# Weight roundings, low parts and loads in another order around the attention's first heads and two graph convolutions, and the second head's up-projection inside the first head

## The chip, the core and the metric

One NeuronCore of a Trainium2 chip runs the whole program. The time is the device time of one execution in microseconds (us), the median over several runs.

## The reference, cut to what matters

x is 256 nodes by 768 features in float32. Four stages follow one another, each `x = x + gnn(layernorm(x))`, `x = x + ffn(layernorm(x))`. Stages 0 and 1 hold a graph attention with 8 heads:

```python
h = (x @ W1).reshape(n, heads, C)            # up-projection, 768 -> 768 for each head
e = leaky_relu(a_s.h[src] + a_d.h[dst])      # edge scores
alpha = segment_softmax(e, dst)
out = segment_sum(h[src] * alpha, dst) + b1  # attention
h = elu(out)
out = gat(h, W2, heads=1)                    # down-projection over all 8 heads, one more attention
```

Stages 2 and 3 hold a graph convolution (`segment_sum((x @ W)[src] * norm, dst) + b`; in stage 3 behind a relational one over 34 edge types). The feed-forward parts of stages 2 and 3 begin with a router, `softmax(x @ router_w + b)`, beside their first weight matrix.

## The kernel before

**Products.** Every float32 product is made of three in a rounded format: hi x hi, lo x hi, hi x lo (`mm3`, L435). For each weight, ACT makes the rounded copy `w_hi` from the loaded `w_in` (`high`, L951), and DVE the low part `w_lo` = `w_in` - `w_hi` (`low`, L1278). PE waits for `w_low`. The same goes for activations: `xT_hi`/`xT_lo`, `h_hi`/`h_lo`, `hid_hi`/`hid_lo`, and the turned attention `aT_hi`/`aT_lo`.

**Weights.** A chunk is a 768 x 768 weight, in two parts of three row tiles. `w_in` holds one chunk: part p of load n is issued on SP (`load`, L301) when ACT and DVE have made `w_hi` and `w_lo` of part p of chunk n-1. `w_hi` and `w_lo` have two halves, which chunks take in turn (`half_of`).

**Attention.** In layer 0 an edge count runs first: a loop of 16 batches in which ACT and DVE build one-hot tiles (L1092, L1511) and PE multiplies them, with head 0's up-projection between. For each head (`gat` on every engine): up-projection into four PSUM banks (12 steps of six 384-column matmuls, tile m and row tile k), scores by four dot products on DVE (L1284), `spread` (PE, waits `scored`: puts the source scores in a row), masked maximum and exponentials on DVE and ACT, normalisation to `alpha`, `turn` (PE, L531, waits `normed`), `aT_hi` on ACT, `aT_lo` on DVE, attention (36 matmuls of 256 columns), ELU in three pieces (`kept`, `exponential`, `rounded` on ACT; `negative`, `unit`, `remainder` on DVE), down-projection (12 steps of 512 + 256 columns). In the loop of heads, PE's order is: up(h), down(h-1) steps 0 to 2, spread(h), down 3 to 8, turn(h), down 9 to 11, attention(h). Head 0 has no down-projection to put between, and fills with matmuls on a tile of zeros (`seed`): 25 between spread and turn, 5 behind the turn. The order on each engine is the order of the code.

**Edge table.** A table of 9.4 MB in DRAM collects edge counts for stage 3. One DMA on SP clears it (L316), and POOL then adds with indirect DMAs (L394), one batch of four a head. For each batch DVE marks first occurrences (`batch_firsts`, L1408, last of them `again`), and waits for POOL to have taken the batch before (`b_taken`, L383).

**Convolutions.** `gcn` (PE): sums over neighbours, then the product with W for tile 0 and tile 1 of the nodes, with the transpositions of tile 0's result (`turn_tile`, L474) before the last two steps of tile 1. On DVE `gcn_out` adds a tile to the stream x (L1702), takes statistics, scales it to `neg_b`; the next product (`gated` in stage 2, `nodes` in stage 3, each with router steps of 8 columns) needs its transposes. The router's weight `rw`, its bias and three to five rows, broadcast by DMAs on ACT's queue (L1177, L1244, L934), all count on one semaphore, for which the rounding of `rw` waits.

## Time and profile before

| | |
|---|---|
| median of 3 runs | 1367.29 us (1366.14 to 1368.6) |
| profiled execution | 1367.41 us, span 1365.6 us, mean granted TensorE clock 0.984 |
| PE busy | 1293.2 us, 95% |
| DVE busy | 995.1 us, 73% |
| ACT busy | 643.3 us, 47% |
| POOL busy | 213.7 us, 16% |
| largest stretch of PE in the chain | 527.50 us, the relation loop |

A page of the profile gives busy times and groups of instructions. Times in the timelines are us from the start of the span. L12 is line 12 of the kernel before. A bracket at the end of a row is the idle time of that engine before it, with what ended it. PE's rows overlap, since matmuls are pipelined.

### The profile page before, as it was taken

The page shows a single profiled execution, that of the slowest core. Times are in us where ns is not written, and L with a number is a line of the kernel's source. Part 1 is how long each engine was busy: PE and PEld are TensorE (multiplying, and loading weights), DVE is VectorE, ACT ScalarE, POOL GpSimd, SP SyncE. Part 2 cuts the span into 40 slices and gives each one's busy share as a digit, 9 for nine tenths or more (in the row PEclk, how much of TensorE's full clock was granted, in tenths as well). Part 3 has the DMA queues.
Part 4 walks back from the last instruction along what each step waited for, and adds up shares of the span by engine and source line. Part 5 has one row for each costly group of instructions (what it writes and reads, how often), then busy time and mean ns, then how long its engine had stood idle before and what let it go on. Part 6 is the DMA issues. An engine that isn't in the chain of part 4 may idle for free.

```text
span 1365.6 us, 21196 instructions
## 1 busy us (share of the span) xinstructions
PE 1293.2 (95%) x7823; PEld 1144.5 (84%) x7823; DVE 995.1 (73%) x1633; ACT 643.3 (47%) x832; POOL 213.7 (16%) x160
## 2 busy tenths in 40 slices
PE   6899999988899999988878999999999999999997
PEld 5699999965799999967667888898888988889886
DVE  6888888987688888975757755666556665566666
ACT  5666565554466555544334433433334333343342
POOL 0034433340034443440000000000000000000200
PEclk9999999998999999998989999999999999999999
DMA  9855665653355665644244554445544455443540
GB/s 303 262 185 169 192 212 174 197 130 120 104 197 169 177 209 191 185 107 132 79 138 162 201 184 154 154 163 192 183 154 154 164 190 183 154 154 139 199 114 32
DMA packets 103875, 227.33 MB, mean 166 GB/s; under 512 B 16710, under 2 KB 34950, under 8 KB 103840
## 3 DMA queue, kind: packets, MB, share of 16 engines
q1 hardware_dynamic: 72924, 192.43, 40.3%
q10 hardware_dynamic: 20980, 31.78, 8.6%
q0 software_dynamic: 9936, 2.66, 2.0%
q8 instruction: 21, 0.34, 0.1%
q14 instruction: 14, 0.11, 0.0%
HBM read 216.56 MB, written 10.29 MB: 166 GB/s over the span
## 4 chain that ended last, share of the span: by engine, by line
PE 82%; DVE 12%; ACT 2%; issue 2%; DMA 2%; ACTq 0%; DVEq 0%; SPq 0%
PE bank L435 80%; DVE w_lo L1278 3%; ACT w_hi L951 1%; DVE stats L1316 1%; PE bank L474 1%; DVE h_lo L1278 1%; PE bank L531 1%; DMA w_in<-L_gnn_W_root 1%; DVE neg_b L1281 1%; DMA x_sb<-x 1%; DVE x_sb L1278 0%; DVE xT_lo L1278 0%; DVE scores_b L1284 0%; DMA hbias_bc<-L_gnn_b_rgcn 0%; DMA w_in<-L_ffn_w 0%
## 5 line engine op out<-in xcount | busy, mean ns | idle before, releaser
L1278 DVE TENSOR_TENSOR w_lo<-w_in,w_hi 128x2304 fp32r<-128x2304 f32 (+4 forms) x162 | 396.4, 2476 | 61.2 <-ACT w_hi L951 61.1
L951 ACT ACTIVATE w_hi<-w_in 128x2304 fp32r<-128x2304 f32 (+4 forms) x162 | 328.4, 2062 | 238.8 <-PE bank L435 203.1
L435 PE MATMUL bank<-w_hi,xT_hi 128*128 128x384 f32 (+3 forms) x942 | 324.3, 344 | 4.7 <-DVE xT_lo L1278 3.0
L435 PE MATMUL bank<-w_lo,xT_hi 128*128 128x384 f32 (+3 forms) x942 | 308.3, 339 | 0.0
L435 PE MATMUL bank<-w_hi,hid_hi 128*128 128x512 f32 (+3 forms) x858 | 293.1, 342 | 5.0 <-DVE hid_lo L1278 4.8
L435 PE MATMUL bank<-w_lo,hid_hi 128*128 128x512 f32 (+3 forms) x858 | 271.3, 337 | 0.0
L435 PE MATMUL bank<-w_hi,xT_lo 128*128 128x384 f32 (+3 forms) x942 | 246.5, 340 | 0.0
L435 PE MATMUL bank<-w_hi,hid_lo 128*128 128x512 f32 (+3 forms) x858 | 224.9, 338 | 0.0
L435 PEld LDWEIGHTS bank<-w_hi,xT_hi 128*128 128x128 f32 (+1 forms) x942 | 178.0, 189 | 31.3 <-issue 4.6
L435 PEld LDWEIGHTS bank<-w_hi,hid_hi 128*128 128x128 f32 (+1 forms) x858 | 161.3, 188 | 41.0 <-issue 6.4
L435 PEld LDWEIGHTS bank<-w_lo,xT_hi 128*128 128x128 f32 (+1 forms) x942 | 177.8, 189 | 13.1
L1807 DVE SCALAR_TENSOR_TENSOR neg_b<-bank,rinv,neg_b 128x512 f32<-128x512 f32 (+1 forms) x136 | 77.4, 611 | 152.7 <-PE bank L435 152.7
L435 PEld LDWEIGHTS bank<-w_lo,hid_hi 128*128 128x128 f32 (+1 forms) x858 | 161.4, 188 | 18.4
L394 POOL DMA_INDIRECT table<-value,row_i x64 | 121.4, 1898 | 245.0 <-DMA table<-value,row_i 226.4
L435 PEld LDWEIGHTS bank<-w_hi,xT_lo 128*128 128x128 f32 (+1 forms) x942 | 157.0, 190 | 1.8
L435 PEld LDWEIGHTS bank<-w_hi,hid_lo 128*128 128x128 f32 (+1 forms) x858 | 134.4, 190 | 1.0
L435 PE MATMUL bank<-aT_hi,h_hi 128*128 128x256 f32 (+1 forms) x408 | 106.4, 280 | 1.9 <-DVE aT_lo L1278 1.9
L435 PE MATMUL bank<-aT_hi,h_lo 128*128 128x256 f32 (+1 forms) x408 | 106.7, 283 | 0.0
L435 PE MATMUL bank<-aT_lo,h_hi 128*128 128x256 f32 x396 | 103.9, 281 | 0.0
L951 ACT ACTIVATE xT_hi<-bank 128x512 fp32r<-128x512 f32 (+1 forms) x85 | 46.9, 563 | 104.2 <-PE bank L435 68.7
L420 POOL DMA_INDIRECT w_in<-L_gnn_W_rel,xrow_i x6 | 7.3, 1211 | 527.6 <-DVE w_lo L1278 526.1
L435 PEld LDWEIGHTS bank<-aT_hi,h_hi 128*128 128x128 f32 x408 | 77.2, 189 | 4.3 <-DVE aT_lo L1278 2.9
(250 smaller groups left out, 1559.2 us busy)
## 6 DMA issues: line engine op xcount, KB each, us to landing
w_in<-L_gnn_W_rel SPq DMA_DIRECT2D x68, 1152.0 KB, 5.7
w_in<-L_gnn_W SPq DMA_DIRECT2D x66, 1152.0 KB, 5.9
table<-zrow SPq DMA_DIRECT2D x1, 9216.0 KB, 31.7
scores_b<-table ACTq DMA_DIRECT2D x34, 256.0 KB, 3.0
a_bc<-L_gnn_a_src ACTq DMA_DIRECT2D x18, 384.0 KB, 3.8
a_bc<-L_gnn_a_dst ACTq DMA_DIRECT2D x18, 384.0 KB, 5.1
key_row<-key_rows ACTq DMA_DIRECT2D x16, 256.0 KB, 5.4
w_in<-ffn_out SPq DMA_DIRECT2D x4, 864.0 KB, 6.6
```

Of the source, the lines that this page charges most:

```text
L394: pool.indirect_dma_start(out=cells, out_offset=bass.IndirectOffsetOnAxis(ap=row_i[:, g:g + 1], axis=0), in_=value[:, g:g + 1], in_offset= ...
L420: pool.indirect_dma_start(out=w_in[:, p, k, :], out_offset=None, in_=t["L3_gnn_W_rel"], in_offset=bass.IndirectOffsetOnAxis(ap=xrow_i[:, 3 ...
L435: return pe.matmul(out, lhsT, rhs, start=start, stop=stop, **kw)
L474: last = pe.transpose(bank[TURNED[i][m][half]][:, k * P:(k + 1) * P], xn[:, m, (3 * half + k) * P:(3 * half + k + 1) * P], ident[:, :])
L531: last = pe.transpose(bank[7][:, sm * N + m * P:sm * N + (m + 1) * P], alpha[:, m, sm * P:(sm + 1) * P], ident[:, :])
L951: act.activation(out, ps, func, **kw).then_inc(mark, 1)
L1278: return dve.tensor_tensor(out, a, b, op)
L1281: return dve.tensor_scalar(out, a, s1, s2, op0, op1) if op1 is not None else dve.tensor_scalar(out, a, s1, None, op0)
L1316: last = dve.bn_stats(stats[:, m, j, :], x_sb[:, m, j * HALF:(j + 1) * HALF])
L1807: last = dve.scalar_tensor_tensor(xs, bank[b][:, c0:c1], weight, xs, mul, add_)
```

## The change

1. **Halves.** In both attentions, W1 of head 0 takes half 0, W1 of the other heads half 1, W2 half 0.
2. **SP.** The clearing DMA becomes four: a quarter behind load 1, two quarters behind load 2 (W1 of head 1), the last behind load 3 (W2 of head 0). POOL waits for all four.
3. **PE.** Head 1's up-projection (`up_second`, 12 steps) goes into head 0. Layer 0: spread, three zero matmuls, 6 steps, turn, three zero matmuls, attention, 6 steps. Layer 1: 2 steps, spread, 6 steps, turn, 1 step, attention, 3 steps. Head 0's attention goes to banks 0, 1, 2. Head 1 then starts with down(0); the loop runs over heads 2 to 7.
4. **ACT and DVE in the attentions.** In layer 0 the weight of head 1 is rounded and its low part made in the edge loop (part 0), and behind `aT_hi`/`aT_lo` (part 1); in layer 1 both parts before head 0. W2's first parts for head 0 follow with part 0 before the ELU and part 1 behind it; the ELU of head 0 takes the interleaved order of the last head. The second edge count on DVE moves from between the maximum and the sums to behind `alpha`.
5. **The bias addition to x** of layer 1 (two instructions, 350.20 in the trace) moves to the end of its attention; layer 0's is there already.
6. **Convolutions.** The row DMAs go ahead of the rounding of the neighbour sums (stage 2) and of the node rows (stage 3). The router's low part and part 1 of the feed-forward weight's low part go between tile 0 and tile 1, in stage 2 the rounding of part 1 too. PE waits for each part of the weight at its first step, not for the chunk.

```diff
                 load(nth(c), dram, SHAPES.get(c, WHOLE))
 
+            def clear(layer, first_, last_):
+
+                if layer == 0:
+                    sp.wait_ge(zeroed, 1)
+                    quarter = ROWS // P // 4
+                    for q in range(first_, last_):
+                        sp.dma_start(table.rearrange("(p t) n -> p t n", p=P)[:, q * quarter:(q + 1) * quarter, :],
+                                     zrow[:, :].unsqueeze(1).to_broadcast([P, quarter, N])).then_inc(cleared, 16)
...
-                if layer == 0:
-
-                    sp.wait_ge(zeroed, 1)
-                    for p in range(2):
-                        sp.wait_ge(w_full[p], 16)
-                    sp.dma_start(table.rearrange("(p t) n -> p t n", p=P),
-                                 zrow[:, :].unsqueeze(1).to_broadcast([P, ROWS // P, N])).then_inc(cleared, 16)
-                with sp.Fori(0, HEADS - 1) as h:
-                    load(h * 2 + (n0 + 2), w1[:, bass.ds((h + 1) * D, D)])
-                    load(h * 2 + (n0 + 3), w2[bass.ds(h * D, D), :])
+                clear(layer, 0, 1)
+                load(n0 + 2, w1[:, D:2 * D])
+                clear(layer, 1, 3)
+                load(n0 + 3, w2[0:D, :])
+                clear(layer, 3, 4)
+                with sp.Fori(0, HEADS - 2) as h:
+                    load(h * 2 + (n0 + 4), w1[:, bass.ds((h + 2) * D, D)])
+                    load(h * 2 + (n0 + 5), w2[bass.ds((h + 1) * D, D), :])
                 load(n0 + 2 * HEADS, w2[(HEADS - 1) * D:HEADS * D, :])
...
+                def up_second(steps):
+
+                    for m, k in steps:
+                        if k == 0:
+                            pe.wait_ge(h_high, 9 * layer * 4 + 2 * m + 2)
+                        if k == 3:
+                            pe.wait_ge(w_low[1], n0 + 3)
+                        last = step_of(m, UP_BANKS[m], k, n0 + 2, 1)
+                        if k == K - 1:
+                            last.then_inc(*((h_mm, 1) if m == 0 else (w_used, 1)))
...
-                up(0, n0 + 1, True)
-
-                spread(9 * layer)
-                if layer == 0:
-                    pe.wait_ge(e_mask, 1)
-                    pe.wait_ge(e_kept, 2)
-                seed((0, 1, 2))
-                seed((0,) * 22)
-                turn(9 * layer)
-                seed((0,) * 5)
-                parts_kept(9 * layer)
-                attend(0)
...
+                if layer == 0:
+                    second = [(m, k) for k0 in (0, 3) for m in range(M) for k in range(k0, k0 + 3)]
+                else:
+                    second = [(m, k) for m in range(M) for k in range(K)]
+                before_spread, before_turn, before_sum = ((0, 6, 6), (2, 8, 9))[layer]
+
+                up_first()
+                up_second(second[:before_spread])
+                spread(9 * layer)
+                if layer == 0:
+                    idle(6, 3)
+                up_second(second[before_spread:before_turn])
+                turn(9 * layer)
+                up_second(second[before_turn:before_sum])
+                if layer == 0:
+                    idle(2, 3)
+                parts_kept(9 * layer)
+                if layer == 0:
+                    pe.wait_ge(e_mask, 1)
+                    pe.wait_ge(e_kept, 2)
+                attend((0, 1, 2))
+                up_second(second[before_sum:])
+                pe.wait_ge(z_kept, 3 * HEADS * layer + 3)
+                seed((0, 1, 2))
+                rest_of(1)
+                with pe.Fori(2, HEADS) as h:
+                    up(h, h * 2 + n0)
+                    rest_of(h)
...
+                    if not first_head:
+                        high(h * 2 + (n0 + 2), h * 2 + (c0 + 3), 1, parts=(0,))
+                    elif layer == 1:
+                        high(n0 + 3, c0 + 4, 0, parts=(0,))
                     attend(u, ahead)
-                    high(h * 2 + (n0 + 2), h * 2 + (c0 + 3), layer, parts=(1,))
+                    if not first_head:
+                        high(h * 2 + (n0 + 2), h * 2 + (c0 + 3), 1, parts=(1,))
+                    elif layer == 0:
+                        high(n0 + 2, 1, 1, parts=(1,))
+                        high(n0 + 3, c0 + 4, 0, parts=(0,))
+                    else:
+                        high(n0 + 3, c0 + 4, 0, parts=(1,))
...
                 deviation(m, m)
                 gcn_rows(0, m)
-            gcn_sums(0)
-            high_chunk(C_FFN2)
             act.dma_start(rw[:, :].rearrange("p (k e) -> p k e", k=K), row_tiles(t["L2_ffn_router_w"], P)).then_inc(ld_mid, 16)
             row_bc(rb[:, :], t["L2_ffn_router_b"], ld_mid)
             row_bc(hbias_bc[:, :], t["L3_gnn_b_rgcn"], ld_mid)
+            gcn_sums(0)
+            high_chunk(C_FFN2, parts=(0,))
             act.wait_ge(ld_mid, LD_MID[2])
             keep(rw_hi[:, :], rw[:, :], rw_high)
 
 
             deviation(0)
             evict_tile(4, 0)
-            high_chunk(C_FFN2 + 1, parts=(0,))
+            high_chunk(C_FFN2, parts=(1,))
             deviation(1)
             evict_tile(4, 1)
-            high_chunk(C_FFN2 + 1, parts=(1,))
+            high_chunk(C_FFN2 + 1)
...
-                    scores(h + 9 * layer, layer, lambda: low(h * 2 + (n0 + 2), layer, parts=(0,)),
-                           begun=first_head and layer == 0, meanwhile=second_count if first_head and layer == 0 else lambda: None)
-                    low(h * 2 + (n0 + 2), layer, parts=(1,))
+                    if first_head:
+                        ahead = second_count if layer == 0 else lambda: None
+                    else:
+                        def ahead():
+                            low(h * 2 + (n0 + 2), 1, parts=(0,))
+
+                    scores(h + 9 * layer, layer, ahead, begun=first_head and layer == 0)
+                    if not first_head or layer == 0:
+                        low(h * 2 + (n0 + 2), 1, parts=(1,))
+                    if first_head:
+                        low(n0 + 3, 0, parts=(0,))
...
-                    if last_head:
+                    if first_head or last_head:
                         negative(0)
...
                         remainder(1)
                         remainder(2)
+                        if first_head:
+                            low(n0 + 3, 0, parts=(1,))
                         batch_firsts(b)
...
+                if layer == 1:
+                    low(n0 + 2, 1)
                 head(0, first_head=True)
...
                 low_chunk(c0 + 18)
-                if layer == 0:
-                    biased(0)
+                biased(layer)
...
                     tile_dots(0, 0, first_out)
                     tile_low(0, 0)
+                if b == 11:
+                    low(2, 1, parts=(0,))
             tile_dots(0, 1, first_out)
...
+            def router_and_second_part(s, c):
+                router_low(s)
+                low_chunk(c, parts=(1,))
+
             low_chunk(C_FFN2, parts=(0,))
-            router_low(0)
-            gcn_out(0, C_GCN2, lambda: low_chunk(C_FFN2, parts=(1,)))
+            gcn_out(0, C_GCN2, lambda: router_and_second_part(0, C_FFN2))
...
             gcn_rows_low(1, 0)
             gcn_rows_low(1, 1)
             gcn_sums_low(1)
-            low_chunk(C_FFN3)
-            router_low(1)
-            gcn_out(1, C_GCN3, lambda: None)
+            low_chunk(C_FFN3, parts=(0,))
+            gcn_out(1, C_GCN3, lambda: router_and_second_part(1, C_FFN3))
```


In the diff, `high(n, free, half, parts)` rounds load n and `low` makes its low part; `low(n0 + 2, 1)` and `low(2, 1, parts=(0,))` are those of head 1's W1.

DVE in the first head of layer 0 (`alpha` is the normalised attention, `w_lo` a weight's low part, `neg_b` the ELU's tile), before:

```order
L1278 TENSOR_TENSOR cnt<-spare 128x512
L1540 MEMSET spare 97x640
L1281 TENSOR_SCALAR alpha<-scores_b,small 128x256 x2
L1278 TENSOR_TENSOR w_lo<-w_in,w_hi 128x2304
L1278 TENSOR_TENSOR aT_lo<-bank,aT_hi 128x512
L1278 TENSOR_TENSOR w_lo<-w_in,w_hi 128x2304
L1281 TENSOR_SCALAR neg_b<-z_b 128x512 x3
L1435 SCALAR_TENSOR_TENSOR neg_b<-neg_b,z_b 128x512 x3
...
L1281 TENSOR_SCALAR again<-first 128x4
L1278 TENSOR_TENSOR hid_lo<-neg_b,hid_hi 128x512 x3
L1278 TENSOR_TENSOR w_lo<-w_in,w_hi 128x2304 x2
```

and with the change:

```order
L1338 TENSOR_SCALAR alpha<-scores_b,small 128x256 x2
L1335 TENSOR_TENSOR cnt<-spare 128x512
L1610 MEMSET spare 97x640
L1335 TENSOR_TENSOR aT_lo<-bank,aT_hi 128x512
L1335 TENSOR_TENSOR w_lo<-w_in,w_hi 128x2304 x2
L1338 TENSOR_SCALAR neg_b<-z_b 128x512 x2
L1499 SCALAR_TENSOR_TENSOR neg_b<-neg_b,z_b 128x512
L1338 TENSOR_SCALAR neg_b<-z_b 128x512
L1499 SCALAR_TENSOR_TENSOR neg_b<-neg_b,z_b 128x512
...
L1335 TENSOR_TENSOR hid_lo<-neg_b,hid_hi 128x512 x2
L1335 TENSOR_TENSOR w_lo<-w_in,w_hi 128x2304
L1464 TENSOR_SCALAR same<-key_row,key 128x128 x4
```

No weight's low part stands between `alpha` and `aT_lo` any more (the second count of 512 columns does), two stand behind `aT_lo`, and a third before the batch's marks.

PE in the same place, from the spread (`ident,scal`) over the turn (`ident,alpha`) to the attention, before:

```order
L435 MATMUL bank<-ident,scal 128x128 x2
L435 MATMUL bank<-zero 128x512 x25
L531 MATMUL bank<-ident,alpha 128x128 x4
L435 MATMUL bank<-zero 128x512 x5
L435 MATMUL bank<-aT_hi,h_hi 128x256
L435 MATMUL bank<-aT_lo,h_hi 128x256
```

and with the change (`...` stands for the rest of six steps like the one shown):

```order
L443 MATMUL bank<-ident,scal 128x128 x2
L443 MATMUL bank<-zero 128x512 x3
L443 MATMUL bank<-w_hi,xT_hi 128x384
L443 MATMUL bank<-w_lo,xT_hi 128x384
L443 MATMUL bank<-w_hi,xT_hi 128x384
...
L539 MATMUL bank<-ident,alpha 128x128 x4
L443 MATMUL bank<-zero 128x512 x3
L443 MATMUL bank<-aT_hi,h_hi 128x256
L443 MATMUL bank<-aT_lo,h_hi 128x256
```

Most of the zero matmuls give way to six steps of the up-projection.

ACT at the convolution of stage 2, between the rounding of the node rows (`h_hi`) and the second tile, before:

```order
L951 ACTIVATE h_hi<-neg_b 128x768
L951 ACTIVATE xT_hi<-bank 128x512 x3
L951 ACTIVATE w_hi<-w_in 128x3x512 x2
L1177 DMA rw<-L_ffn_router_w 128x6x8
L934 DMA rb<-L_ffn_router_b 128x8
L934 DMA hbias_bc<-L_gnn_b_rgcn 128x768
L951 ACTIVATE rw_hi<-rw 128x48
L951 ACTIVATE std<-mv 128x1
L951 ACTIVATE xT_hi<-bank 128x3x128 x2
L951 ACTIVATE w_hi<-w_in 128x3x512
```

and with the change:

```order
L991 ACTIVATE h_hi<-neg_b 128x768
L1232 DMA rw<-L_ffn_router_w 128x6x8
L974 DMA rb<-L_ffn_router_b 128x8
L974 DMA hbias_bc<-L_gnn_b_rgcn 128x768
L991 ACTIVATE xT_hi<-bank 128x512 x3
L991 ACTIVATE w_hi<-w_in 128x3x512
L991 ACTIVATE rw_hi<-rw 128x48
L991 ACTIVATE std<-mv 128x1
L991 ACTIVATE xT_hi<-bank 128x3x128 x2
L991 ACTIVATE w_hi<-w_in 128x3x512
```

The three DMAs pass the roundings of `xT` and of both weight parts, and one of the weight's parts (128x3x512) goes behind tile 0's.

## Rows read from the trace of the kernel before

**Rows 1.** The page's section 4: the chain that ended last, by engine.
```profile
PE 82%; DVE 12%; ACT 2%; issue 2%; DMA 2%; ACTq 0%; DVEq 0%; SPq 0%
```

**Rows 2.** The chain of waits in order of time: start us, us, engine and what.
```profile
57.83 2.46 DVE w_lo L1278
...
60.95 27.14 PE bank L435 x166
88.53 30.06 PE bank L435 x184
...
369.38 27.13 PE bank L435 x166
397.02 30.12 PE bank L435 x184
...
686.45 5.03 DMA hbias_bc<-L_gnn_b_rgcn
```

**Rows 3.** Timeline of DVE, first head of layer 0: start us, us, operation, [idle before].
```profile
41.66 0.30 DVE L1278 TENSOR_TENSOR spare<-iota,edge_f 128x136 bf16<-128x136 bf16 x1 [0.77 <-PE bank L435]
...
54.81 0.68 DVE L1278 TENSOR_TENSOR cnt<-spare 128x512 f32<-128x512 f32 x1
...
66.97 1.89 DVE L1435 SCALAR_TENSOR_TENSOR neg_b<-neg_b,z_b 128x512 f32<-128x512 f32 x3
...
77.50 0.16 DVE L1423 COPY b_head<-b1c 128x6 f32 x1
...
80.05 0.96 DVE L1284 CUSTOM_DVE_ANT_0 spare<-z_b,a_bc 128x768 f32<-128x768 f32 x1 [0.16 <-DVE scal L1284]
```

**Rows 4.** Timeline of PE, the first turn of layer 0.
```profile
57.89 0.66 PE L531 MATMUL bank<-ident,alpha 128*128 128x128 f32 x4 [3.31 <-DVE alpha L1281]
```

**Rows 5.** Timeline of DVE, second head of layer 1: third of its four dot products.
```profile
388.48 0.96 DVE L1284 CUSTOM_DVE_ANT_0 spare<-z_b,a_bc 128x768 f32<-128x768 f32 x1 [0.16 <-DVE scal L1284]
```

**Rows 6.** Timelines of ACT, DVE and PE around the convolution of stage 2.
```profile
672.72 0.84 ACT L951 ACTIVATE h_hi<-neg_b 128x768 fp32r<-128x768 f32 x1 [0.95 <-DVE neg_b L1281]
...
691.50 0.24 ACT L951 ACTIVATE rw_hi<-rw 128x48 fp32r<-128x48 f32 x1 [4.58 <-DMA hbias_bc<-L_gnn_b_rgcn]
...
691.77 0.21 DVE L1278 TENSOR_TENSOR rw_lo<-rw,rw_hi 128x48 fp32r<-128x48 f32 x1 [7.45 <-ACT rw_hi L951]
691.90 1.14 DVE L1702 SCALAR_TENSOR_TENSOR x_sb<-bank,dinv,x_sb 128x512 f32<-128x512 f32 x2
...
695.54 1.54 PE L474 MATMUL bank<-ident,neg_b 128*128 128x128 f32 x6 [7.06 <-DVE neg_b L1281]
...
705.13 0.81 PE L474 MATMUL bank<-ident,neg_b 128*128 128x128 f32 x6
```

**Rows 7.** Windows behind the convolutions' gaps: busy us (instructions), then granted clock, DMA share, GB/s.
```profile
695.50:702.50 7.00, 6.96 (x28) 6.24 (x29) 4.29 (x6) 2.47 (x3) 0.00 (x0) 0.59 0.15 31
1314.40:1320.00 5.60, 5.60 (x26) 5.02 (x27) 2.31 (x5) 2.20 (x3) 0.00 (x0) 0.70 0.44 101
```

**Rows 8.** Timelines of ACT and PE around the convolution of stage 3.
```profile
1303.53 4.15 ACT L951 ACTIVATE w_hi<-w_in 128x2304 fp32r<-128x2304 f32 x2 [1.94 <-issue]
...
1314.39 0.87 PE L474 MATMUL bank<-ident,neg_b 128*128 128x128 f32 x6 [2.64 <-DVE neg_b L1281]
...
1324.29 0.82 PE L474 MATMUL bank<-ident,neg_b 128*128 128x128 f32 x6
```

**Rows 9.** The page's section 6: the clearing of the table, KB and us to landing.
```profile
table<-zrow SPq DMA_DIRECT2D x1, 9216.0 KB, 31.7
```

**Rows 10.** Timeline of POOL: the start of the first three batches.
```profile
70.93 0.56 POOL L382 TENSOR_TENSOR value<-first,ones 128x4 f32<-128x4 f32 x1 [21.93 <-DVE again L1281]
...
103.83 1.80 POOL L382 TENSOR_TENSOR value<-first,ones 128x4 f32<-128x4 f32 x1 [1.51 <-DMA table<-value,row_i]
105.60 2.51 POOL L383 TENSOR_TENSOR row_f<-spill,again 128x4 f32<-128x4 f32 x1
...
134.44 1.67 POOL L382 TENSOR_TENSOR value<-first,ones 128x4 f32<-128x4 f32 x1 [1.64 <-DMA table<-value,row_i]
```

More of the change, by code:

```diff
@@ L539, in gat, with step_of @@
                 c0, n0, b0 = C_GAT[layer], NTH_GAT[layer], layer * HEADS
[L541 to L554 removed]
+                def step_of(m, banks, k, n, half, first=False):
+                    if m == 0 and k % 3 == 0:
+                        pe.wait_ge(w_low[k // 3], n + 1)
+                    if first:
+                        of_tile(2 * layer, m)(k)
+                    return mm3([(bank[banks[j]][:, 0:HALF], part(w_hi, w_lo, slice(0, P), half, k, slice(j * HALF, (j + 1) * HALF)))
+                                for j in range(2)],
+                               part(xT_hi, xT_lo, slice(0, P), k, slice(m * P, (m + 1) * P)), k == 0, k == K - 1)
@@ L555, in up, with up_first @@
+                def up_first():
+                    if between is not None:
+                        between(lambda m, banks, k: step_of(m, banks, k, n0 + 1, 0, True))
                         return
-                    for m, banks in ((0, (5, 6)), (1, (3, 4))):
-                        if not first:
-                            pe.wait_ge(z_kept, (h + HEADS * layer) * 3 + (-2 if m == 0 else 0))
+                    for m in range(M):
                         for k in range(K):
-                            last = step_of(m, banks, k)
-                        last.then_inc(*((h_mm, 1) if m == 0 else (w_used, 2 if first else 1)))
+                            last = step_of(m, UP_BANKS[m], k, n0 + 1, 0, True)
+                        last.then_inc(*((h_mm, 1) if m == 0 else (w_used, 2)))
@@ new lines, in up @@
+                def up(h, n):
+                    for m in range(M):
+                        pe.wait_ge(z_kept, (h + HEADS * layer) * 3 + (-2 if m == 0 else 0))
+                        for k in range(K):
+                            last = step_of(m, UP_BANKS[m], k, n, 1)
+                        last.then_inc(*((h_mm, 1) if m == 0 else (w_used, 1)))
[7 more added lines that the diff above has]
+                        if k == K - 1:
+                            last.then_inc(*((h_mm, 1) if m == 0 else (w_used, 1)))
@@ L785, in both @@
                 def both(k):
+                    if m == 0 and k % 3 == 0:
+                        pe.wait_ge(w_low[k // 3], nth(C_FFN2 if s == 2 else C_FFN3) + 1)
                     ready(k)
@@ L1022, in kept @@
                         for k in (2 * j, 2 * j + 1):
-                            last = act.activation(z_b[:, k, :], bank[(5, 3, 4)[j]][:, (k % 2) * N:(k % 2 + 1) * N], ACT.Identity,
+                            last = act.activation(z_b[:, k, :], bank[((0, 1, 2) if first_head else (5, 3, 4))[j]][:, (k % 2) * N:(k % 2 + 1) * N], ACT.Identity,
                                                   bias=b1_head[:, k:k + 1])
@@ L1097, in _ @@
                     keep_tile(0, h_hi, h_high)
+                if b == 7:
+                    high(2, 1, 1, parts=(0,))
                 if b == 11:
@@ L1459, in head @@
                             remainder(j)
-                        low(h * 2 + (n0 + 3), 1 - layer)
+                    if not first_head and not last_head:
+                        low(h * 2 + (n0 + 3), 0)
+                if layer == 1:
+                    low(n0 + 2, 1)
                 head(0, first_head=True)
```

75 lines of the change are left out of this document (33 added, 42 removed).

## Prediction

> **What bounds the kernel now.** I read the page's chain by engine first [rows 1]: TensorE (PE) holds 82% of it, DVE 12%. So the time is PE's own work plus the places where PE stands still, and those are short. The chain in order of time [rows 2] shows them: after each long PE segment look at what stands between it and the next. In the first head of layer 0 it is a low part at 57.83 and, behind it, the low part of the turned attention, up to 60.95; in the first convolution a bias row, 5.03 us from issue to landing. The timelines by engine give the causes. The profiled run took 1367.41 us, 0.12 above the median of 1367.29, so a sum against it stands for the median too. No change can be told from change within 0.2%, 2.7 us.
>
> **Layer 0, first head.** PE waits out the scores under 25 and 5 zero matmuls and still stands 3.31 us [rows 4]. The change puts 12 steps of head 1's up-projection there. What is a step worth? A head is 64,512 columns (attention 9,216, up and down 27,648 each) in 30.06 us [rows 2], so a step of 2,304 columns takes 1.07 us, attention 4.3. Twelve steps are 12.9 us of PE work out of the way; but DVE must deliver everything earlier, and I find that it can't.
> Head 0: one low part, 2.5 us (as at 57.83 in [rows 2]), goes into the edge-counting loop, where 0.77 us of DVE's time is free [rows 3]: +1.7. The second edge count (0.68 at 54.81 [rows 3], with the clearing of its tile, about as long, some 1.3 in all) leaves the chain of scores for the time after alpha: -1.3. Alpha is ready 0.4 later, but no low part stands before the turned one any more: 1.3 of counting lies beside the turn instead of 2.5, and attention starts at about 60.3, not 60.95.
> Then PE has attention 4.3, six steps 6.4, and three down steps with their seeds 3.6: it reaches the spread of head 1 at 74.6. DVE has, from 60.3: a 1.3 wait for the rounding, two low parts (to 66.6), the ELU in interleaved order (9 operations, those at 66.97 took 0.63 each [rows 3], about 5.5 with waits: 72.1), a wait for the last rounding 1.5, its low part (to 76.0), the batch's first marks 2.0 (before, from the last of the ELU's three at 68.86 [rows 3] to POOL's start at 70.93 [rows 10]). So it starts head 1 at 78.0 instead of 77.50 [rows 3], and its third dot product, for which the spread waits and which ended at 81.01 [rows 3], ends at 81.5, 3.5 behind the start as before. **PE stands 6.9 us**: the hidden steps come back as a stall. From the spread to the end of the turn before was 81.07 to 88.53 [rows 2], 7.46 of DVE's and ACT's chain; PE's own work there (spread 0.5, six down steps 6.4) just fits under it. At full clock the turn ends at 88.95: +0.4.
> The clock: after 7.06 us of idle PE its granted clock was 0.59 over the next 7.0 us, after 2.64 it was 0.70 over 5.6 [rows 7] (1.00 is 2.4 GHz, 0.50 is 1.2): 2.9 and 1.7 us lost, while the segment behind layer 0's gap of 3.31 us [rows 4] took 27.14 us, as long as the same one of layer 1 behind 0.6 (27.13) [rows 2]: no loss there. So a stall of this length can cost nothing or 2.9. I take 2.5, since 6.9 is nearest to 7.06, less 0.1 of slack: +2.4. Layer 0: **+2.8**. The Trainium skill ("TensorE: Matmul & The Clock Gate", Part 1: The HAM clock gate) has the throttled clock as the default to which the array falls back when it idles, so it speaks against a change that trades zero matmuls for a longer stall. By it the drop is certain and the sum stays 1356.4; by the 3.31 us gap alone it would be 1351.8. The clocks of [rows 7] agree with the page, that gap doesn't.
>
> **Layer 1, first head.** The same, but both low parts of W1 for head 1 are made before head 0, in the boundary, where the bias addition also left (1.8); and one low part fewer stands after the attention. Attention starts about 0.4 earlier; DVE then needs a low part, the ELU, a low part and the marks, and head 1's third dot ends at 385.9 instead of 389.44 (388.48 + 0.96 [rows 5]): -3.5. PE reaches that spread at 380.1 and stands 5.7 us. Clock loss 2.5, less 0.3 of slack to the turn (389.4 to 397.02 [rows 2] is 7.6, PE needs 7.3): +2.2. Layer 1: **-1.3**. The later heads keep their period: same operations, other halves.
>
> **Convolution of stage 2.** DVE ends the first low part of the FFN's weight at 684.3 and stands 7.45 us, until 691.77 [rows 6], for the rounding of the router's weight (691.50), which waits for the bias row that is issued at 686.45 [rows 2] behind both roundings of w_in. The change issues the three rows right after ACT's 672.72 rounding: issue 1.4 us, 5.03 to land, there by 680. The first tile then starts behind that low part, at 684.4, its normalised rows are there 3.6 later (from 691.90 to PE's turn at 695.54 [rows 6]), at 688.0; PE is busy with the product until 688.5 (695.54 less 7.06; two steps of it stand behind the turn), so the gap of 7.06 us is gone and with it the slow stretch (2.9). The DVE order matters for the second tile: the low part of part 1 (its rounding now ends about 691.4) to 693.2, then 3.6: its turn at 696.8, where it was 705.13. **-8.3**; nothing behind it up to the relation loop waits for a transfer that this brings nearer by more than its slack.
>
> **Convolution of stage 3.** Five row DMAs leave the place before the roundings (1.94 us of issue), and one low part of 2.5 and the router's leave the place before tile 0. Together they would give 4.5, but the first tile's product ends only at 1307.4 (PE's gap begins at 1314.39 less 2.64, and four steps of the second tile lie before it), so tile 0 starts at 1307.5, not 3.6 before its turn at 1314.39 [rows 8], and the turn comes at 1311.7, when PE is free: -2.7. No gap, no slow stretch (1.7, of which some 1.5 lay before the second tile's turn at 1324.29 [rows 8]): that turn comes at about 1320.1. DVE has the second tile ready by then: tile 0 to 1311.1, its low parts and the weight's second part to 1316, 3.6 for the tile. **-4.2**.
>
> **The quartered clear.** 9.2 MB in one DMA take 31.7 us [rows 9]; in quarters of 7.9 the last is issued behind a load that waits for a low part at 64.1. I cost it at nothing: what hides it is POOL's slack, see the last rival. The Trainium skill ("DMA: Bandwidth & Descriptors", "Issuing engines are not separate DMA queues") says all queues end on the same 16 engines; by it the quarter would also hold up the load behind it: 1359.4, the third rival. No row here has a load and the clear on two queues.
>
> Sum: +2.8 -1.3 -8.3 -4.2 = **-11.0: 1356.4 us**.
>
> **Rivals.**
> - *The clock holds* in both first heads, as after the 3.31 us gap: minus 2.4 and 2.2, 1351.8 us. For: that row. Against: gaps of 2.64 and 7.06 dropped. Chance 0.15.
> - *The clock stays low longer*, 10 us instead of the 5 or so behind 2.5: another 2.5 each, 1361.4. The mean of 0.59 over 7 us bounds it only for that place. 0.13.
> - *A load comes late.* Head 2's first W1 part is issued at about 66.6 behind the last quarter's 7.9 us and lands near 80 to 84; ACT must round it before head 1's exponentials at about 85. Up to 3 us: 1359.4. 0.08.
> - *The convolutions give half*: tile 1 stays where it was because something else than the row held it; minus 6.2 instead of 12.5, 1362.7. Against: DVE's 7.45 us of idleness with one named releaser. 0.07.
> - *DVE does not bind*: then the hidden steps count in full: six steps (6.4) in layer 0, nine (9.6) in layer 1 instead of +2.8 and -1.3, 1338.9. Only if my DVE list is wrong by 7 us. 0.04.
> - *Slower: the series of indirect adds runs late.* POOL's first batch started at 70.93 [rows 10]; now the last quarter lands about 76, POOL's dump add follows, and the batch starts at 83.5, 12.6 late. DVE's marks of batch b wait until POOL took batch b-1 (for batch 1 the two operations from 103.83 end at 108.1; the marks of batch 2 need that at about 131, two periods of 30.5 behind the first: 23 us of slack, 10 left). Over the five further heads it bites if a batch takes over 32.6 us, and outweighs the gain from about 35.3; at 36 it costs 17: 1373. For: the first batch took 32.9. Against: the next took 30.6 [rows 10], the heads' own pace, and DVE never waited for it. 0.04.
> The forecast itself has 0.49.
>
> **How the numbers follow.** The predicted time is the forecast's, 1356.4. The range reaches down past the first rival's 1351.8 to 1350.5 (the stall 1.3 shorter in one head) and up past 1361.4 to 1362.7, the half gain: it leaves out the full gain, the slow case and misses of several terms at once. All cases but the last are faster than 1364.7, 0.2% below the profiled run; some of the slow case's chance, and a combination of late load, long slow clock and half gain, lies near 1367. Faster 0.93, same 0.03, slower 0.04.
>
> **What the next profile should show.** PE idle for 5 to 7 us before head 1's spread in both layers, ended by DVE's scal; granted clock near 0.5 to 0.7 behind it; marks of the first batch near 77; no gap of PE before either turn in the convolutions, and the relation loop starting about 6.8 us earlier (2.8 - 1.3 - 8.3). I am wrong if PE runs through head 1's spread, if tile 0 of stage 2 starts after 688, or if DVE's marks wait for POOL.

## The result, and the profile after

The changed kernel takes 1358.12 us in the median of 4 runs (1354.77 to 1359.37), the kernel before in the same set 1367.94 (1366.14 to 1368.88). The ratio is 0.9919, 95% interval 0.9896 to 0.9941: 11 us less, between 8 and 14. (The changes in us are worked out from the ratio; the two medians lie 9.8 us apart.) In a later set of runs it was 0.9916 (0.9900 to 0.9932). The profiled execution took 1354.77 us (span 1352.9), 12.6 less than the profiled one of before, and is the fastest of its four; the other three had a mean granted clock of 0.982 to 0.984, this one 0.986.

The page of the changed kernel, busy times and the chain by engine:

```profile
PE 1281.9 (95%) x7775; PEld 1138.7 (84%) x7775; DVE 995.6 (74%) x1633; ACT 642.6 (47%) x832; POOL 209.4 (15%) x160
...
PE 82%; DVE 11%; ACT 3%; issue 2%; DMA 1%; DVEq 0%; ACTq 0%; SPq 0%
```

PE's share of the chain is what it was [rows 1]; PE is busy 11.3 us less. Most of that is zero matmuls: 179 of them instead of 227, and 30 take 6.65 us in an experiment below, so 48 are about 10.6 us. The chain of waits in order of time (start us, us, what), then for the kernel before a line of its chain and a line of PE's timeline:

```profile
61.37 5.03 DVE w_lo L1335 x2
...
90.58 30.09 PE bank L443 x184
...
397.40 30.12 PE bank L443 x184
...
749.74 527.50 PE bank L443 x3264
```

```profile
758.74 527.50 PE bank L435 x3264
...
680.85 0.50 PE L435 MATMUL bank<-w_hi,xT_hi 128*128 128x512 f32 x1 [0.44 <-DVE w_lo L1278]
```

Read the starts against each other. Head 1's turn of layer 0 ends 2.05 us late (90.58 against 88.53 [rows 2]), that of layer 1 only 0.38 late (397.40 against 397.02), and the relation loop of 527.50 us starts 9.0 early (749.74 against 758.74). The gain lies between 397 and 750, and behind the loop.

PE in the two first heads, then around the two convolutions, in the changed kernel:

```profile
58.03 0.66 PE L539 MATMUL bank<-ident,alpha 128*128 128x128 f32 x4 [0.99 <-DVE alpha L1338]
...
60.17 0.38 PE L443 MATMUL bank<-aT_hi,h_hi 128*128 128x256 f32 x1 [0.84 <-DVE aT_lo L1335]
...
81.58 1.22 PE L443 MATMUL bank<-ident,scal 128*128 128x128 f32 x4 [6.74 <-DVE scal L1341]
...
388.12 1.22 PE L443 MATMUL bank<-ident,scal 128*128 128x128 f32 x4 [5.86 <-DVE scal L1341]
...
679.76 0.50 PE L443 MATMUL bank<-w_hi,xT_hi 128*128 128x512 f32 x1 [0.46 <-DVE w_lo L1335]
...
687.24 0.82 PE L482 MATMUL bank<-ident,neg_b 128*128 128x128 f32 x6
...
695.36 0.87 PE L482 MATMUL bank<-ident,neg_b 128*128 128x128 f32 x6 [1.08 <-DVE neg_b L1338]
...
1302.59 0.82 PE L482 MATMUL bank<-ident,neg_b 128*128 128x128 f32 x6
...
1310.86 0.82 PE L482 MATMUL bank<-ident,neg_b 128*128 128x128 f32 x6
```

The brackets carry it: PE now stands 6.74 us before head 1's spread in layer 0 (81.58) and 5.86 us in layer 1 (388.12), each time for DVE's `scal`. Before, it ran through both. The 7.06 and 2.64 us gaps before the turns of tile 0 [rows 6, 8] are gone (687.24 and 1302.59 have no bracket). From PE's restart in the stage 2 product (679.76, before 680.85) to the second tile's turn (695.36, before 705.13) it takes 15.60 us instead of 24.28: -8.7. From the start of the relation loop to the same turn of stage 3 (1310.86; before 1324.29 [rows 8]) it takes 561.12 us instead of 565.55: -4.4.

DVE in the first head of layer 0 and in stage 2, and ACT's router rounding:

```profile
61.37 5.03 DVE L1335 TENSOR_TENSOR w_lo<-w_in,w_hi 128x2304 fp32r<-128x2304 f32 x2 [1.25 <-ACT w_hi L991]
...
73.40 2.56 DVE L1335 TENSOR_TENSOR w_lo<-w_in,w_hi 128x2304 fp32r<-128x2304 f32 x1 [1.43 <-ACT w_hi L991]
...
80.56 0.96 DVE L1341 CUSTOM_DVE_ANT_0 spare<-z_b,a_bc 128x768 f32<-128x768 f32 x1 [0.16 <-DVE scal L1341]
...
683.23 1.14 DVE L1772 SCALAR_TENSOR_TENSOR x_sb<-bank,dinv,x_sb 128x512 f32<-128x512 f32 x2
...
677.78 0.23 ACT L991 ACTIVATE rw_hi<-rw 128x48 fp32r<-128x48 f32 x1
```

DVE works from 61.37 to the dot product at 80.56 almost without a pause. It waits twice for ACT's rounding of a weight (1.25 us ahead of 61.37, 1.43 us ahead of 73.40); its other waits there are under 0.4 us each. In stage 2 the router's rounding is done at 678.0, not 691.7, and tile 0 starts at 683.23.

### The profile page after: what moved, and what is told of

The parts are those of the page before. It is cut to its first block, busy times and chain, and to the rows that moved or that the text cites. A ratio compares the mean times of both kernels' runs of the same rounds, so it can differ in the third digit from the quotient of the medians.

```text
span 1352.9 us, 21068 instructions
## 1 busy us (share of the span) xinstructions
PE 1281.9 (95%) x7775; PEld 1138.7 (84%) x7775; DVE 995.6 (74%) x1633; ACT 642.6 (47%) x832; POOL 209.4 (15%) x160
## 4 chain that ended last, share of the span: by engine, by line
PE 82%; DVE 11%; ACT 3%; issue 2%; DMA 1%; DVEq 0%; ACTq 0%; SPq 0%
PE bank L443 81%; DVE w_lo L1335 3%; ACT w_hi L991 1%; DVE stats L1373 1%; PE bank L539 1%; PE bank L482 1%; DMA w_in<-L_gnn_W_root 1%; DVE h_lo L1335 1%; DMA x_sb<-x 1%; DVE neg_b L1338 0%; DVE xT_lo L1335 0%; DVE x_sb L1335 0%; DMA scores_b<-table 0%; DVE neg_b L1579 0%; ACT xT_hi L991 0%
```

## The experiments

All ratios are to the kernel before, run in the same set, with 95% intervals; 0.1% is 1.37 us.

**One part at a time.** Four kernels in one set. The convolutions alone:

```diff
 (kernel before)
+ point 6 of the change, both stages; nothing of points 1 to 5
```

> The kernel before with the reordering around both convolutions alone (points 6 of the change). Theory A (all of the gain is in the convolutions, the attention part nets about nothing): the changed kernel's profile showed -8.6 and -4.4 us at the two places, so 12 to 13 us less than before, about 1355, slightly below the full change. Rival B (both parts contribute alike): about 6 us less, 1362.

Measured: 0.9924 (0.9903 to 0.9944), -10.4 us. The attention's part alone:

```diff
 (full change)
- point 6 of the change
```

> The full change with both convolutions put back as before: halves, quartered clear, head 1's up-projection and the first head's orders stay. Theory A: head 1's turn ends +2.1 late in layer 0 and +0.4 in layer 1 (cumulated), so 0 to 1 us slower than before, 1367.5 to 1369. Rival B: the hidden steps pay, 4 to 6 us less than before, about 1363.

Measured: 1.0004 (0.9989 to 1.0020), +0.5 us. Its chain has head 1's turns at

```profile
91.61 30.05 PE bank L443 x184
...
399.96 30.06 PE bank L443 x184
```

that is 3.1 and 2.9 us later than before. Both say the same: half of the gain or more in the attention part, as the two rivals had it, lies outside both intervals, and the convolutions give the gain within the noise. Head 1's 12 hidden steps bring nothing that can be measured: between 1.5 us less and 2.7 us more.

```diff
 (kernel before)
+ point 6, stage 2 alone
```

> The kernel before with the reordering around the convolution of stage 2 alone. Theory A: the 7.06 us gap of PE before the turn goes and the slow stretch behind it (2.9 lost) too; -8.5 us, about 1359.5. Rival: the place is followed by a wait for the load of the root weight, which was 7.3 us in the chain; if that load holds, less than 5 us are left at the end.

Measured: 0.9935 (0.9915 to 0.9954), -8.9 us. The rival, the wait for the root weight's load, takes nothing of it.

```diff
 (kernel before)
+ point 6, stage 3 alone
```

> The kernel before with the reordering around the convolution of stage 3 alone. Theory A: the 2.64 us gap goes and its slow stretch (1.7): -4.3 us, about 1363.5. Rival: only the gap goes (-2.7, 1365), because the slow stretch comes from something else or comes back later in the tail.

Measured: 0.9970 (0.9957 to 0.9983), -4.1 us; its second tile's turn comes at 1322.22, and the relation loop in that execution began at 761.07: 561.15 us from one to the other, the full change's figure. The interval (2.3 to 5.9 us less) holds theory A's 4.3 and the rival's 2.7 alike, so the times don't decide between them; the trace, with 4.4 less, is for theory A. The two stages alone add up to 13.0, together they gave 10.4; the intervals are 4 to 6 us wide, so this is no contradiction and no proof of a loss.

**Two causes in stage 2.** Only the three DMAs move:

```diff
+            act.dma_start(rw[:, :].rearrange("p (k e) -> p k e", k=K), row_tiles(t["L2_ffn_router_w"], P)).then_inc(ld_mid, 16)
+            row_bc(rb[:, :], t["L2_ffn_router_b"], ld_mid)
+            row_bc(hbias_bc[:, :], t["L3_gnn_b_rgcn"], ld_mid)
             gcn_sums(0)
             high_chunk(C_FFN2)
-            act.dma_start(rw[:, :].rearrange("p (k e) -> p k e", k=K), row_tiles(t["L2_ffn_router_w"], P)).then_inc(ld_mid, 16)
-            row_bc(rb[:, :], t["L2_ffn_router_b"], ld_mid)
-            row_bc(hbias_bc[:, :], t["L3_gnn_b_rgcn"], ld_mid)
```

> The kernel before; only the three row DMAs of stage 2 are issued ahead of the rounding of the neighbour sums. Theory A (two causes at this place): the router's rounding then waits for the second weight part, whose load landed at 685.4, so tile 0 starts near 687.2 instead of 691.9, PE keeps a gap of 2 to 2.5 us before the turn, and the gain is about 5 us of the 8.9 that the whole reordering of this place gave; 1362. Rival B (the bias row alone is the cause): all 8.9, 1358.

Measured: 0.9955 (0.9939 to 0.9971), -6.1 us. PE around the turns, and DVE:

```profile
680.26 0.50 PE L435 MATMUL bank<-w_hi,xT_hi 128*128 128x512 f32 x1 [0.45 <-DVE w_lo L1278]
...
690.39 0.88 PE L474 MATMUL bank<-ident,neg_b 128*128 128x128 f32 x6 [2.51 <-DVE neg_b L1281]
...
698.49 0.82 PE L474 MATMUL bank<-ident,neg_b 128*128 128x128 f32 x6
...
686.62 0.21 DVE L1278 TENSOR_TENSOR rw_lo<-rw,rw_hi 128x48 fp32r<-128x48 f32 x1 [2.89 <-ACT rw_hi L951]
```

The gap has shrunk to 2.51 us, and DVE still waits 2.89 us for the router's rounding, now behind the second weight part. From PE's restart (680.26) to the second turn it is 18.23 us: 6.05 of the 8.7 come from the rows, 2.6 from the new order of parts. By the times alone this could not be told from the whole reordering of stage 2, whose interval (0.9915 to 0.9954) overlaps this one.

**What the clock costs in that gap.**

```diff
                     if k == 4:
-                        turn_tile(i, 0)
+                        turn_tile(i, 0, 30 if s == 0 else 0)
```

> The kernel before; 30 matmuls on the tile of zeros stand in PE's 7.06 us gap before the turn of stage 2, nothing else. Theory A (PE's idleness brings the clock down): no slow stretch behind the gap, -2.5 to -2.9 us, about 1364.5, granted clock 1.00 in the 7 us behind. Rival B (the clock's fall has another cause, a power or data one): no change, 1367.

Measured: 0.9982 (0.9970 to 0.9993), -2.5 us, with the waits of before. PE and the window behind:

```profile
686.92 6.65 PE L435 MATMUL bank<-zero 128*128 128x512 bf16 x30
694.26 0.87 PE L474 MATMUL bank<-ident,neg_b 128*128 128x128 f32 x6 [0.68 <-DVE neg_b L1281]
...
698.15 0.24 PE L435 MATMUL bank<-rw_hi,xT_hi 128*128 128x8 f32 x1 [0.93 <-issue]
...
702.34 0.82 PE L474 MATMUL bank<-ident,neg_b 128*128 128x128 f32 x6
```

```profile
694.00:701.00 7.00, 5.81 (x35) 5.03 (x36) 5.46 (x11) 2.56 (x4) 0.00 (x0) 1.00 0.25 49
```

Granted clock 1.00 (2.4 GHz) where it was 0.59 [rows 7]. From the first turn to the second it takes 8.08 us, before 9.59 (695.54 to 705.13 [rows 6]). So PE's idleness did bring the clock down: the clock was low (0.59 to 0.69) behind this gap in all three profiles that have it, and not in this one. In these traces 1.5 of the 2.9 us lost lay on the path to that turn. The rest was hidden: at full clock PE stands 0.93 us before the router's step at 698.15, just behind the end of DVE's low part (698.05), and at the low clock it reached that step too late to wait. The 8.7 us of this place are 7.06 of gap and about 1.5 of clock.

**Is it DVE that sets head 1's spread?**

```diff
                         remainder(1)
                         remainder(2)
+                        batch_firsts(b)
                         if first_head:
                             low(n0 + 3, 0, parts=(1,))
-                        batch_firsts(b)
```

> The full change; in both first heads DVE makes the batch's marks before the low part of W2's second part, not behind it. Theory A (DVE's chain sets head 1's spread): the marks fill the 1.43 us wait for ACT's rounding in layer 0, the spread comes 1.4 us earlier, PE's stall is 5.3 instead of 6.7 us; in layer 1 there is no such wait and nothing changes; about -1.4 us against the full change, 1356.5. Rival B (PE waits there for something else as well): no change, 1358.

Measured: 0.9903 (0.9885 to 0.9921), against 0.9919 and 0.9916 of the full change; too close to tell by the times. The trace tells:

```profile
80.37 1.22 PE L443 MATMUL bank<-ident,scal 128*128 128x128 f32 x4 [5.60 <-DVE scal L1341]
...
388.15 1.22 PE L443 MATMUL bank<-ident,scal 128*128 128x128 f32 x4 [5.69 <-DVE scal L1341]
```

The spread comes 1.2 us earlier in layer 0 (80.37 against 81.58), at the same place in layer 1, as DVE's chain has it. Its turn ended at 89.97, only 0.6 earlier: from spread to turn it took 9.60 us instead of 9.00, with a granted clock of 0.50 over the first 4 us instead of 0.57.

**Does that stall cost twice?**

```diff
                     down(h - 1, h * 2 + (n0 + 1), 0, 3)
+                    idle(7, fill)
                     spread(h + 9 * layer)
-                rest_of(1)
+                rest_of(1, (27, 22)[layer])
```

> The full change; 27 (layer 0) and 22 (layer 1) matmuls on the tile of zeros stand before head 1's spread, where PE stood 6.74 and 5.86 us. Theory A (the stall costs twice, once as idleness of PE and once by the clock): granted clock 1.00 behind both, head 1's turn ends 1.3 and 1.6 us earlier, -2.9 us against the full change, 1355. Rival B (the slack before the turn hides the slow stretch): less than 1 us, 1357.5.

Measured: 0.9895 (0.9876 to 0.9913), -3.3 us against the full change of the first set. The two intervals overlap, so the time agrees with theory A without proving it; the trace decides. Chain and windows behind the two spreads:

```profile
89.43 30.02 PE bank L443 x184
...
394.56 30.06 PE bank L443 x184
...
82.00:86.00 4.00, 4.00 (x25) 3.53 (x25) 3.90 (x8) 1.35 (x2) 0.00 (x0) 1.00 0.09 18
387.00:391.00 4.00, 3.96 (x24) 3.53 (x25) 3.88 (x7) 0.00 (x0) 1.44 (x1) 1.00 0.14 8
```

and the windows of the full change at the same places:

```profile
81.50:85.50 4.00, 3.92 (x15) 3.50 (x16) 3.86 (x9) 0.74 (x1) 0.00 (x0) 0.57 0.15 42
388.00:392.00 4.00, 3.88 (x13) 3.40 (x14) 3.86 (x9) 0.00 (x0) 1.84 (x2) 0.50 0.12 8
```

Clock 0.57 and 0.50 become 1.00; the turn of layer 0 ends at 89.43 although the zeros delayed the spread from 81.58 to 82.05, and the first head of layer 1 (from its own spread to head 1's turn) takes 33.82 us (394.56 - 360.74) instead of 35.59 (397.40 - 361.81). The stall does cost twice. Four profiles of the attention part have no zeros there, three have them. From the start of head 1's spread to the end of its turn PE takes 9.00 to 10.26 us in layer 0 without them and 7.38 to 7.48 with them; in layer 1 it is 8.99 to 9.34 and 7.49 to 7.52. Against the mean with zeros the low clock costs 1.6 to 2.8 us behind the stall of layer 0 and 1.5 to 1.8 behind that of layer 1.

**One more set, with controls.**

> The full change once more, beside the three kernels after it, so that a few us between them can be told. 9 to 12 us less than before.

Measured: 0.9916 (0.9900 to 0.9932). Its profile shows a longer stall in layer 0 than the first one (7.73 us, not 6.74), and ACT shows why:

```profile
72.09 2.13 ACT L991 ACTIVATE w_hi<-w_in 128x2304 fp32r<-128x2304 f32 x1 [0.99 <-DMA w_in<-L_gnn_W]
...
82.43 1.22 PE L443 MATMUL bank<-ident,scal 128*128 128x128 f32 x4 [7.73 <-DVE scal L1341]
```

The rounding of W2's second part waited 0.99 us for its load, and DVE waited 2.42 us for that rounding instead of 1.43. The load was issued at 63.86, 0.4 us ahead of the last quarter of the clear, and landed 8.1 us later; in the first profile (64.00) it took 7.2. Head 1's turn ends at 91.62, 3.1 us later than before.

> The convolutions' reordering alone once more, in the same set. Theory A (the attention part nets nothing): within 2 us of the full change. Rival B: the full change is 3 us or more ahead.

Measured: 0.9904 (0.9891 to 0.9917). Again the convolutions alone are as good as the full change, within their intervals (1.6 us ahead of it by the ratios).

```diff
 (full change; marks first and idle(7, fill) as in the two experiments above)
+                rest_of(1, (21, 21)[layer])
```

> The full change with the marks first, and 21 zero matmuls before head 1's spread in both layers. Theory A (DVE's chain and the clock are two separate costs): both gains add, -1.4 and -2.9, so 4 us less than the full change and 3 to 4 less than the convolutions alone. Rival B (they are the same stall, seen twice): no more than the better of the two, 3 us less than the full change.

Measured: 0.9895 (0.9880 to 0.9910), -2.9 us against the full change, no more than the zeros alone gave in the other set, and 1.2 ahead of the convolutions alone, where theory A had 3 to 4. Its turns end at 88.16 and 393.12, 1.3 and 1.4 before those with the zeros alone: the gain of layer 0, carried on to layer 1. So the traces are for theory A, the times fit rival B better, and the intervals (4 us wide) can't decide.

```diff
 (the kernel with marks first and zeros, now 17 and 21 of them instead of 21 and 21)
                     elif layer == 1:
                         high(n0 + 3, c0 + 4, 0, parts=(0,))
+                    else:
+                        high(n0 + 2, 1, 1, parts=(1,))
                     attend(u, ahead)
...
                     elif layer == 0:
-                        high(n0 + 2, 1, 1, parts=(1,))
                         high(n0 + 3, c0 + 4, 0, parts=(0,))
```

> As the kernel before it in this set; in layer 0 ACT rounds part 1 of head 1's weight before head 0's exponentials, where it stood idle 4.09 us, not behind the turn. Theory A (DVE's chain): its 1.25 us wait for that rounding goes, so head 1's spread comes 1.2 us earlier, about -1.2 us more. Rival B: the next wait grows by as much (ACT's rounding of W2's second part, or the load of it, which is issued only when the low part before is made), no change.

Measured: 1351.19 us, 0.9872 (0.9857 to 0.9887), -17.5 us: the fastest of all, 6 us ahead of the full change in its set and 3.1 ahead of the kernel with marks first and zeros, where 1.2 was expected; all four of its runs lie below all five of that kernel's. The four zeros fewer in layer 0 are a second edit, whose effect was not separated. DVE with the late and with the early rounding:

```profile
61.55 5.03 DVE L1336 TENSOR_TENSOR w_lo<-w_in,w_hi 128x2304 fp32r<-128x2304 f32 x2 [1.25 <-ACT w_hi L992]
...
74.62 2.56 DVE L1336 TENSOR_TENSOR w_lo<-w_in,w_hi 128x2304 fp32r<-128x2304 f32 x1 [0.51 <-ACT w_hi L992]
...
79.66 0.96 DVE L1342 CUSTOM_DVE_ANT_0 spare<-z_b,a_bc 128x768 f32<-128x768 f32 x1 [0.16 <-DVE scal L1342]
```

```profile
60.01 5.01 DVE L1337 TENSOR_TENSOR w_lo<-w_in,w_hi 128x2304 fp32r<-128x2304 f32 x2
...
72.47 2.55 DVE L1337 TENSOR_TENSOR w_lo<-w_in,w_hi 128x2304 fp32r<-128x2304 f32 x1
...
77.50 0.96 DVE L1343 CUSTOM_DVE_ANT_0 spare<-z_b,a_bc 128x768 f32<-128x768 f32 x1 [0.16 <-DVE scal L1343]
...
85.97 30.05 PE bank L443 x184
```

Both brackets are gone (1.25 and 0.51), and the third dot product is 2.2 us earlier, not 1.2. Rival B expected the second wait to grow; it went too. With the late rounding ACT had waited 1.03 us for the load of W2's second part, issued at 64.18 and landed 8.2 us later; with the early one that load was issued at 62.63, since DVE was done with the part before it sooner, landed in 6.6 us, and ACT did not wait. Head 1's turn ends at 85.97, 2.6 us earlier than in the kernel before (88.53 [rows 2]) and 2.2 earlier than with the late rounding (88.16). The profiled executions lie 3.6 us apart; the 1.4 us beyond the 2.2 arise in places that the two edits don't touch. That rounding was ready to be made: ACT stood idle 4.09 us before head 0's exponentials in the changed kernel.

## Why the prediction was right

- **Layer 0's first head** (predicted +2.8): +2.05 in the first profile, +3.1 with the convolutions undone and +3.1 in the second profile of the full change. In the first profile the DVE list held to tenths: attention at 60.17 (predicted 60.3), third dot ending at 81.52 (81.5), a stall of 6.74 us (6.9). In the second the load came 1 us later than DVE could have used it, and the stall was 7.73. The experiment with the marks first confirms that DVE's chain sets the spread.
- **Layer 1's** (predicted -1.3): -1.67 in the first pair of profiles, from +2.05 to +0.38. That pair was a favourable draw. From head 1's turn of layer 0 to that of layer 1, before-style attention takes 308.3 to 310.2 us in seven profiles, the changed one without added zeros 306.8 to 308.4 in four; the means lie 1.4 apart. The third dot ended at 388.05; from the start of attention (370.72) it is 17.3 us, before 20.1 (369.38 to 389.44). The stall was 5.86 us (predicted 5.7).
- **The clock term** was set a little too high. I took 2.5 us for each stall, 2.4 and 2.2 with the slack taken off. In the first pair of profiles it was 1.6 in layer 0 and 1.8 in layer 1, in all four profiles 1.6 to 2.8 and 1.5 to 1.8. The size had been read from the 7.06 us gap of stage 2, where 2.9 us of rate were lost but only 1.5 on the path. The Trainium skill ("TensorE: Matmul & The Clock Gate", Part 1: The HAM clock gate) has the throttled clock as the state to which the array falls back when it idles. The zero matmuls in both places, with the clock at 1.00 behind them and DVE's chain as it was, agree, so this objection to the change was sound, by 1.5 to 2.8 us a stall. The prediction held the 3.31 us gap against it; the last section shows that the clock was low behind that same gap in four of seven profiles. The segment of 27.14 us that the prediction read there starts at 60.95, 3.06 us behind the end of the gap, and could show no slow stretch ahead of that.
- **Stage 2** (predicted -8.3): -8.7 in the traces, -8.9 alone. Tile 0 started at 683.23, 1.1 earlier than predicted because PE and DVE were there 1.1 earlier too. The prediction priced gap and clock together; the runs split it in 7.06 and 1.5 by cause and in 6.1 and 2.6 by edit. The first cause was deeper than the row alone: with the rows out of the way DVE still waited 2.89 us for the router's rounding, behind that of the weight's second part.
- **Stage 3** (predicted -4.2): -4.4, -4.1 alone. The product's end, not DVE, held the first tile, as worked out: DVE's bracket at tile 0 was 1.39 us, released by PE. The share of the clock in it (1.6 in the profile of before) depends on the execution: see the last section.
- **The sum.** The predicted terms give -11.0, and the ratio -11. That they meet within tenths is luck: the interval is 8 to 14 us, the two parts measured alone gave +0.5 and -10.4 (-13.1 in the later set) where the terms have +1.5 and -12.5. The relation loop starts 9.0 us early, not 6.8. Of the profiled pair's -12.6, 1.5 us arise between 397 and 680. The bias addition of layer 1 now stands there (598.22), but that stretch takes 282.7 to 286.5 us in the seven profiles of before-style attention and 282.4 to 285.0 in those of the changed one, so 1.5 us can't be ascribed to it; 1.5 us are lost again in two places behind the convolutions.
- **The rivals.** The clock did not hold, nor stay low for 10 us. The load of head 2's weight came late by 3.69 us of ACT's time (its rounding waited until 80.11), but was done at 82.2, before the exponentials at 85.79: no cost. The load that did cost was another, W2's second part for head 0. The slow case's first half came true and its second did not (its bound for outweighing the gain should have been 34.8 us a batch, 32.6 and a fifth of the 11.0, not 35.3):

```profile
78.20 1.76 POOL L414 DMA_INDIRECT table<-zrow,dump_i  x1 [74.28 <-DMA table<-zrow]
86.73 0.29 POOL L390 TENSOR_TENSOR value<-first,ones 128x4 f32<-128x4 f32 x1 [6.76 <-DMA table<-zrow,dump_i]
...
113.70 0.91 POOL L390 TENSOR_TENSOR value<-first,ones 128x4 f32<-128x4 f32 x1 [4.64 <-DMA table<-value,row_i]
```

POOL's first batch started 15.8 us late (86.73 against 70.93 [rows 10]; 12.6 predicted), but it then took 27.0 us, not 32.9, and the next one 23.1 (113.70 to 136.76): the adds can go faster than the heads need them, and the third batch started only 2.3 us late. DVE never waited for POOL. So the late end of the clear costs nothing. Whether its last quarter costs something on the other side stays open: the load issued just ahead of it took 6.6 to 8.2 us to land in seven profiles, two loads at about the same place before took 7.3 and 6.7, and in three of the seven (8.1 to 8.2) ACT waited about 1 us for it. A kernel with the clear alone undone was not tried.

## What to carry to other kernels

Before work is moved into an engine's wait, list what the engine that it waits for must now deliver earlier; if that list fills the time, the moved work comes back as a stall at the next hand-over, and the stall may cost again in clock. DMAs that fill small tables belong ahead of the first thing that their issuing engine waits for, and a semaphore shared by several loads makes the least needed one bind. A wait that is left is the next place to look: the rounding that ACT could have made in its idle time was worth 2.2 us in the trace, more than all twelve hidden steps. A wait that can't be removed can at least be filled with matmuls on a tile of zeros, if they end before what is waited for arrives; here that took 1.5 to 2.8 us off what followed each long stall.

## What was not expected

A short gap, in the same code, sometimes brings the clock down and sometimes not. Behind layer 0's 3.31 us gap before the first turn, two executions of before-style attention read, in the kernel before and in the first profile of the convolutions alone (the window from 57 to 62 us):

```profile
57.00:62.00 5.00, 2.78 (x17) 1.92 (x18) 4.62 (x6) 2.61 (x2) 0.00 (x0) 1.00 0.80 113
```

```profile
58.04 1.12 PE L531 MATMUL bank<-ident,alpha 128*128 128x128 f32 x4 [3.31 <-DVE alpha L1281]
...
57.00:62.00 5.00, 3.96 (x15) 2.35 (x16) 4.15 (x8) 2.61 (x2) 0.00 (x0) 0.66 0.53 113
```

Of seven profiles with this gap three have 1.00 and four 0.66. The gap of stage 3 does the same. In the experiment with zeros in stage 2's gap, which leaves stage 3 as it was, it kept the clock, where the kernel before had 0.70 [rows 7]:

```profile
1311.78 0.87 PE L474 MATMUL bank<-ident,neg_b 128*128 128x128 f32 x6 [2.65 <-DVE neg_b L1281]
...
1311.80:1317.40 5.60, 5.60 (x38) 5.10 (x38) 3.40 (x7) 3.15 (x4) 0.00 (x0) 1.00 0.39 95
```

The same at four kinds of place, over the fourteen profiles of this document (granted clock over the 4 to 7 us from about the end of each gap):

| PE's gap | gaps | granted clock behind it |
|---|---|---|
| 2.6 us, ahead of stage 2's neighbour sums | 14 | 1.00 in twelve, 0.71 in two |
| 2.5 to 2.9 us, ahead of a first tile's turn | 6 | 1.00 in two, 0.50 to 0.70 in four |
| 3.3 us, first turn of layer 0 | 7 | 1.00 in three, 0.66 in four |
| 5.2 to 7.7 us, head 1's spreads and stage 2 | 11 | 0.50 to 0.69 in all |

Whether a slow stretch costs time depends on what runs in it. Behind the 3.31 us gap it hits the five zero matmuls, which take about 2.3 us instead of 1.24 and end about when attention can start anyway: from the turn to attention it is 3.06 or 3.07 us in all seven, and head 1's spread comes at most 0.3 us later. So the price of that place was close to nothing even where the clock fell. In stage 3 it hits the product, and from the first tile's turn to the second's it takes 9.89 to 11.09 us in the four profiles with the low clock, 8.32 in the one without. Ahead of stage 2's neighbour sums it hits those sums, and from them to the product it takes 7.52 or 7.53 us in the two profiles instead of 6.24 in the kernel before.

The scatter between runs goes with the clock too. Of 22 executions of the kernel before in one set, the two with a mean granted clock of 0.978 and 0.979 took 1371.7 and 1372.6 us, and the thirteen with 0.985 or more 1364.8 to 1368.3. Only the profiled executions show places; in them the low clock cost 1.3 us ahead of stage 2's product and 1.6 to 2.8 in stage 3 where it came, and the rest of the scatter stays open. The Trainium skill (the same page and part) calls the number of cold matmuls, those at the low clock, run-variable, as counted at a kernel's start; these traces show the like behind gaps inside a kernel. Single profiled pairs of this kernel should not be compared closer than a few us.
